# Attention and experts on one core: x loaded by columns, layer norm's scale applied to q on VectorE, no transposes of x

## What is computed

```
q = layernorm(x) @ W_q.T + b_q          k, v = ctx @ W_k.T + b_k, ctx @ W_v.T + b_v
attn = softmax(q k / 4) per head        x = x + (attn v) @ W_out.T + b_out
logits = layernorm(x) @ Wr + br         two best experts, gates = softmax of their logits
x = x + sum over the two of gate * ((silu(x_n W1a + b1a) * (x_n W1g + b1g)) @ W2 + b2)
```

## Time and profile before

| | us |
|---|---|
| median of 3 runs | 1176.52 (1175.81 to 1178.37) |
| the profiled execution | 1174.99 |
| its span, first to last instruction | 1173.2 |
| PE busy | 1136.0 (97%) |
| DVE busy | 941.5 (80%) |
| ACT busy | 774.8 (66%) |
| POOL busy | 597.5 (51%) |
| first scores (slot 0) | starts at 24.86 |
| slot 4 to slot 55 | 52.91 to 457.87 |
| expert part, all of it | about 530 to 1173 |

### The profile page before, as it was taken

One profiled execution on the slowest core, in us unless ns is written; L12 is line 12 of the kernel. 1 busy time (PEld: TensorE's weight loads), 2 busy tenths in 40 slices (PEclk: granted clock), 3 DMA queues, 4 the chain that ended last, 5 costly groups with the idle time before them and its releaser, 6 DMA issues. The chain is left out here.

```text
span 1173.2 us, 38427 instructions
## 1 busy us (share of the span) xinstructions
PE 1136.0 (97%) x12514; PEld 1018.2 (87%) x12515; DVE 941.5 (80%) x2949; ACT 774.8 (66%) x1635; POOL 597.5 (51%) x729
## 2 busy tenths in 40 slices
PE   6999999999999999988999999999999999999995
PEld 4677777777777777777999999999999999999995
DVE  6789999999999999898888877776776777677772
ACT  5677777777777776666766766666666666666652
POOL 6345677767766776595564333333333333333333
PEclk9999999999999999999999999999999999999998
DMA  5123333333333333536787776777777777767743
GB/s 191 36 74 94 110 106 100 113 113 104 104 109 113 111 102 105 188 127 215 191 221 201 200 212 171 217 195 190 189 210 200 172 198 210 192 172 214 194 109 68
DMA packets 106631, 180.18 MB, mean 154 GB/s; under 512 B 14400, under 2 KB 80128, under 8 KB 106368
## 3 DMA queue, kind: packets, MB, share of 16 engines
q1 hardware_dynamic: 74448, 136.54, 36.4%
q0 software_dynamic: 25584, 35.54, 16.0%
q10 hardware_dynamic: 6464, 6.36, 1.7%
HBM read 132.57 MB, written 45.29 MB: 152 GB/s over the span
## 5 line engine op out<-in xcount | busy, mean ns | idle before, releaser
L1782 POOL DMA_INDIRECT out_rows<-y_gated,block_tokens x114 | 187.2, 1642 | 257.3 <-DMA out_rows<-y_gated,block_tokens 107.4
L675 PE MATMUL bank<-block_T_hi,w_hi 128*128 128x256 f32 x912 | 261.1, 286 | 0.7 <-DVE block_T_lo L1397 0.7
L677 PE MATMUL bank<-block_T_hi,w_lo 128*128 128x256 f32 x912 | 256.1, 281 | 0.0
L676 PE MATMUL bank<-block_T_lo,w_hi 128*128 128x256 f32 x912 | 256.1, 281 | 0.0
L839 ACT ACTIVATE probs_T<-bank 128x512 f32<-128x512 f32 x256 | 132.1, 603 | 64.7 <-PE bank L512 64.7
L675 PEld LDWEIGHTS bank<-block_T_hi,w_hi 128*128 128x128 f32 x912 | 173.9, 191 | 0.9 <-DVE block_T_lo L1397 0.9
L676 PEld LDWEIGHTS bank<-block_T_lo,w_hi 128*128 128x128 f32 x912 | 173.2, 190 | 0.0
L677 PEld LDWEIGHTS bank<-block_T_hi,w_lo 128*128 128x128 f32 x912 | 172.9, 190 | 0.0
L1095 DVE TENSOR_REDUCE row_max<-bank 128x4 f32<-128x512 f32 x256 | 157.9, 675 | 13.0 <-PE bank L493 13.0
L1715 POOL DMA_INDIRECT routed_rows<-rows,dest_i x128 | 129.7, 1013 | 37.3 <-issue 33.4
L1380 DVE TENSOR_TENSOR w_lo<-w_raw,w_hi 128x1024 fp32r<-128x1024 f32 x114 | 134.1, 1218 | 6.2 <-ACT w_hi L940 6.2
(11 more groups left out here) (211 smaller groups left out, 2941.0 us busy)
## 6 DMA issues: line engine op xcount, KB each, us to landing
w_raw<-in_L_ffn_W SPq DMA_DIRECT2D x114, 512.0 KB, 4.7
half_w<-in_L_ffn_W SPq DMA_DIRECT2D x42, 512.0 KB, 5.6
block_rows<-routed_rows SPq DMA_DIRECT2D x57, 272.0 KB, 4.8
x_in<-in_x SPq DMA_DIRECT2D x64, 128.0 KB, 2.4
ctx_T<-in_ctx SPq DMA_DIRECT2D x16, 512.0 KB, 4.5
x_res<-in_x SPq DMA_DIRECT2D x64, 128.0 KB, 2.6
out_rows<-x SPq DMA_DIRECT2D x64, 128.0 KB, 2.3
w_lo<-in_L_ffn_W ACTq DMA_DIRECT2D x8, 512.0 KB, 4.4
```

Of the source, the lines that this page charges most:

```text
L675: mm(dst, w1h[k][:, c, at:at + P], xh[:, k, c, :], start=(c == 0), stop=False)
L676: mm(dst, w1h[k][:, c, at:at + P], xl[:, k, c, :], start=False, stop=False)
L677: last = mm(dst, w1l[k][:, c, at:at + P], xh[:, k, c, :], start=False, stop=(c == KC - 1))
L1782: nc.gpsimd.indirect_dma_start(out=out[:, :], out_offset=bass.IndirectOffsetOnAxis(ap=tk[:, u % U, t:t + 1], axis=0), in_=yg[:, u % 2, t, ...
```

## The change

- The host also lays x out by columns (`x_T`, as the context already is). Per group one DMA brings 512 KB (`load_xt`, q = 3). `xn`, `ln1_norm`, `to_T` and the transposes are gone. x by rows is still loaded, for the statistics alone.
- `xT_hi(g, c)`: two ACT casts of 128x512 per group (q = 3 and q = 1) in place of four of 128x256. `xT_lo(g, c)`: two DVE subtractions of 128x512, SBUF to SBUF, in slots q = 2 and 3, in place of four of 128x256.
- The mean is taken out of W_q once: two matmuls against a tile of 1/256, one DVE subtraction. rstd is applied behind the projection: `q_scaled(g, o)` on DVE, 128x512, PSUM times a row of rstd copied to all partitions, in slots q = 0 and 1; then ACT adds the bias in place at the end of the slot (`q_bias`).
- rstd goes through DRAM to become a row: SP stores 128x4 numbers at q = 0 (`store_rstd`) and loads them to 128 partitions at q = 1 (`load_rstd`). `rb` is then read with a step of four numbers (16 bytes).
- `rstd1` on POOL is one instruction instead of three. `ln1_stats` and `rstd1` stand at q = 2 and 3 instead of q = 1 and 3.
- `before()` is in another order on every engine.

```diff
+        def store_rstd(eng, g):
+            eng.wait_ge(s_rs1, 2 * (g + 1))
...
+            eng.dma_start(rr[g].rearrange("(p q) -> p q", p=P), rs1[:, g % 2, :]).then_inc(s_rst, 16)
+        def load_rstd(eng, g):
...
+            eng.dma_start(rb[:, g % 2, :], rr[g].rearrange("(o n) -> o n", o=1).to_broadcast([P, GB * P])).then_inc(s_rld, 16)
...
+                if t % GB == 0 and real(t + 2 * GB):
+                    store_rstd(sp, t // GB + 2)
+                if t % GB == 1 and real(t + 2 * GB):
+                    load_rstd(sp, t // GB + 2)
+                if t % GB == 3 and real(t + 4 * GB):
+                    load_xt(t // GB + 4)
...
-                if real(t + 9):
-                    pe.wait_ge(s_xl, t + 9)
-                    to_T(t + 9, bank[6])
...
+            def q_bias(g, o):
+                act.wait_ge(s_qm, 2 * g + o + 1)
+                dst = qT0[:, g % 3, :] if o == 0 else qT1[:, g % 2, :]
+                nc.scalar.activation(dst, dst, ACT.Identity, bias=bqc[:, o:o + 1]).then_inc(s_ev, 1)
...
+            def q_scaled(g, o, bk):
+                dve.wait_ge(s_qk, GB * g + o + 1)
+                dve.wait_ge(s_rld, (g + 1) * 16)
...
+                V.tensor_tensor(dst.rearrange("m (q p) -> m q p", q=GB), bk[:, :].rearrange("m (q p) -> m q p", q=GB),
+                                rb[:, g % 2, :].rearrange("m (p q) -> m q p", q=GB), ALU.mult).then_inc(s_qm, 1)
...
-                if real(t + 8):
-                    xT_lo(t + 8, bank[6])
+                if q < 2 and real(GB * (t // GB + 1)):
+                    q_scaled(t // GB + 1, q, bank[5])
+                if q >= 2 and real(GB * (t // GB + 2)):
+                    xT_lo(t // GB + 2, q - 2)
...
-                if t % 2 == 1 and real(t + 11):
+                if q == 2 and real(t + 10):
+                    ln1_stats(t + 10)
+                if q == 3 and real(t + 11):
                     ln1_stats(t + 11)
```

More of the change, by code:

```diff
@@ L451, in split3 @@
                 return last
-            def to_T(t, bk):
-                pe.wait_ge(s_xn, count(t))
-                for c in range(KC):
-                    last = nc.tensor.transpose(bk[:, c * P:(c + 1) * P], xn[:, t % LB, c * P:(c + 1) * P], ident)
-                last.then_inc(s_xT, 1)
             def qk_proj(g, o, bk):
@@ L536, in before @@
             def before():
-                pe.wait_ge(s_const, 16)
-                for q in range(GB):
-                    to_T(q, bank[q])
-                pe.wait_ge(s_wl, 2)
-                for o in range(4):
-                    qk_proj(0, o, bank[4 + o])
-                for q in range(GB):
-                    pe.wait_ge(s_xl, q + 1)
-                    to_T(GB + q, bank[q])
-                pe.wait_ge(s_wl, 4)
-                for q in range(GB):
-                    pe.wait_ge(s_ev, q + 1)
-                    v_proj(q, bank[4 + q])
-                pe.wait_ge(s_v, GB)
-                pe.wait_ge(s_xl, LB)
+                pe.wait_ge(s_zro, 1)
+                pe.wait_ge(s_wn[0], 16)
+                for c in range(KC):
+                    last = mm(bank[3][:, 0:D], avg[:], w_in[:, 0, c, :], start=(c == 0), stop=(c == KC - 1))
+                last.then_inc(s_wm, 1)
+                for o in range(4):
+                    if o % 2 == 0:
+                        pe.wait_ge(s_wl, o // 2 + 1)
+                    qk_proj(0, o, bank[4 + o])
+                pe.wait_ge(s_wl, 3)
+                for q in (2, 3, 0, 1):
+                    if q < 2:
+                        pe.wait_ge(s_qm, q + 1)
+                    else:
+                        pe.wait_ge(s_ev, q - 1)
+                    v_proj(q, bank[4 + q])
+                pe.wait_ge(s_const, 16)
             def squares_and_out(t):
@@ L604, in slot @@
                 if t == 0:
-                    to_T(LB, bank[6])
+                    pe.wait_ge(s_v, GB)
                     pe.wait_ge(s_bvr, 1)
+                    pe.wait_ge(s_wl, 4)
                     for c in range(KC):
@@ L891, in slot @@
                     nc.scalar.activation(nT[:].rearrange("p c n -> p (c n)"), bank[4][:, 0:D], ACT.Copy).then_inc(s_nT, 1)
-                if real(GB * g):
-                    qk_out(g, q, bank[5])
+                if real(GB * g) and q >= 2:
+                    k_out(g, q, bank[5])
                 if q == 0 and real(t - 8):
@@ L1191, in before @@
                 ln1_stats(2)
+                dve.wait_ge(s_wm, 1)
+                V.tensor_tensor(w_in[:, 0], w_in[:, 0],
+                                bank[3][:, 0:D].rearrange("p (o n) -> p o n", o=1).to_broadcast([P, KC, D]),
+                                ALU.subtract).then_inc(s_wc, 1)
+                for c in range(KC):
+                    xT_lo(0, c)
+                dve.wait_ge(s_wc, 1)
+                w_part_lo(0)
+                w_part_lo(1)
                 dve.wait_ge(s_const, 16)
@@ L1196, in before @@
                 last.then_inc(s_bke, 1)
-                w_part_lo(0)
-                w_part_lo(1)
-                for q in range(GB):
-                    xT_lo(q, bank[q])
+                w_part_lo(2)
                 ln1_stats(4)
-                w_part_lo(2)
                 ln1_stats(6)
+                for o in range(2):
+                    q_scaled(0, o, bank[4 + o])
+                for c in range(KC):
+                    xT_lo(1, c)
+                ln1_stats(LB)
                 w_part_lo(3)
-                ln1_stats(LB)
                 V.tensor_copy(tri_bf[:], consts[:, C_TRI:C_TRI + P])
@@ L1213, in before @@
                 last.then_inc(s_bvr, 1)
-                for q in range(GB):
-                    xT_lo(GB + q, bank[q])
                 ln1_stats(LB + 2)
```

187 lines of the change are left out of this document (102 added, 85 removed).

## The result

The changed kernel takes 1203.31 us (median of 4 runs, 1201.28 to 1204.49), the kernel before 1177.44 us (4 runs): 1.0222 times as long, 95% interval 1.0202 to 1.0242. The profiled execution took 1203.02 us, its span 1201.1 against 1173.2 us. So the span grew by 27.9 us; the prediction had put 3.9.

A forecast was written before the change was run, and what follows sets the result against it. It took PE's work and ACT's exponentials to end each slot together, with DVE nearly late at q = 0. -0.5 + 2.9 + 0.5 + 1.0 = +3.9 us on 1176.52 gave 1180.4 us, range 1175.5 to 1187.5.

The forecast's parts named there:

- PE's transposes, -0.01 us a slot: Steady slots: without PE's transposes the exponentials end the slot, 7.75 instead of 7.76 us; about -0.5 us over 51 slots.
- `q_scaled`, 0.69 us: DVE, slots q = 0 and 1: 689 ns for 128x512, 0.27 us more than what it replaces, if the step costs nothing.
- rival 1: Slots q = 0 and 1: the stepped rstd read makes `q_scaled` 1218 ns, +6 us, 1186.4 in all; chance 0.15.
- PE now has 0.46 us to give before `pv` 3: Slots q = 0 and 1: `q_scaled` delays x2, `v_proj` is 0.1 us late, and PE's spare time covers it: nothing.
- Slots q = 0, +0.24 at L507: Twelve slots q = 0 (8 to 52): DVE's maxima end 0.27 us later, L507 comes 0.24 us later; +2.9 us.
- Slots q = 1, "punctual" after losing the statistics: DVE, slots q = 1: about 1.5 us of statistics leave, 0.27 comes; its end is 1.2 us earlier, q = 2 starts punctual.
- q = 2 takes the statistics: DVE, slots q = 2: 1.5 us of statistics go into 1.60 us of idle time; taken as nothing.
- rival 2: SP's queue: maxima's rows come late behind the x_T load or rstd's store, +5.2 us, 1185.6 in all; chance 0.10.
- The start, +1.0 us: First slots: maxima of tile 0 at 26.1 to 28.4, so slots come 0 to 2.3 us later; +1.0 taken.
- Rival 3: The start gains what PE's first projection gains, some 3.5 to 4 us: 1175.6 in all; chance 0.14.
- Slots 56 and 57, +0.5: Slots 56 and 57 get two `q_scaled` where DVE is already late: about +0.5 us over three slots.
- Expert part, 0: Expert part at the end: same code and order, so no change, 0 us.

The follow-up runs named there:

- Experiment 5: Router's matmuls and ranks behind the transposed scores: changed kernel with rstd row ordered and POOL waiting, 1.0110; statistics moved too, 1.0109; kernel before, 1.0063.
- e2: Changed kernel, POOL in slots q = 0 waiting with its low part of the context until VectorE's four additions are done: 1.0152 times the kernel before.
- e11: Changed kernel with ACT copying the rstd row into order once per group and POOL waiting for the additions: 1.0139 times the kernel before, 1193.67 us.
- experiment 6: Addresses of W1's first-buffer tiles: kernel before with 64 bytes free ahead of them, 1.0053; changed kernel with them at the old addresses, 1.0084.
- e14: Kernel before with one unused 64-byte tile ahead of `w1_raw0`: 1.0053 times the kernel before.

## Why the prediction was wrong, point by point

- **PE's transposes, -0.01 us a slot.** Right, and with it the reading that the exponentials end the slot: q = 2 and 3 take 7.76 us, with the two waits of 0.3 us before `pv` 2 and 3. Experiment 5 adds that this holds for this order of PE only.
- **`q_scaled`, 0.69 us.** Mis-sized: 1.08, measured with and without the step (1076 and 691 ns). It lay between the bounds of 0.417 and 1.218, and I had taken "the row of its own size". This was rival 1's condition (over 0.95 us), chance 0.15. The Trainium skill ("Advanced Engine Details and Errata", SBUF Cachelines) speaks of a penalty where accesses each hit another 16-byte cacheline, and gives no figure; here it is 0.385 us over 512 numbers in each partition. (Rival 1's "0.65 us after `v_proj` could start" is 0.62 by the reckoning that made 0.27 us into 0.1 late; nothing hangs on it.)
- **What waits for it.** The step "PE now has 0.46 us to give before `pv` 3", so that only `v_proj` counts, failed. `pv` 0 waits for the addition of the logits (for q = 1 also for that of the ranks), which stands behind `q_scaled` on VectorE. Rival 1 priced the two slots at 0.42 us together with 0.65 us of lateness; slots q = 0 lost 0.2, and of the 0.94 us of slots q = 1 0.24 are lost behind L534.
- **Slots q = 0, +0.24 at L507.** The length was right by accident (7.96 us; "7.95 to 8.05"), its place wrong: L534 comes on time. q = 3 did not end 0.27 us later, because its last small instruction (`ln_var_eps`) takes 0.17 us and no longer 0.45: in the kernel before it stood at 333.61, just ahead of the row of 333.98 in the earlier trace rows, and ended with a POOL instruction (333.31 to 334.03).
- **Slots q = 1, "punctual" after losing the statistics.** This is the step that failed most: 11.9 of the 14.4 us. Its block transpose starts 1.59 us behind PE, for VectorE's slot q = 0 takes 8.79 instead of 7.14 us: 0.66 from `q_scaled` (1.08 - 0.42) and 0.92 from the two additions that stand behind POOL. That the statistics are gone from its own end does not help, since it is late at its start. No rival had the additions in it. One of these slots, 17, owes some 1.1 of its 2.05 us to the lower clock (below).
- **q = 2 takes the statistics.** Right: 7.76 us.
- **SP, the x_T load, the DMAs of rstd (rival 2).** Nearly right. In slots 4 to 55 one wait of L534 is for the DMA of the maxima, where the kernel before has none:

```profile
262.82 0.10 PEld L534 LDWEIGHTS bank<-minus_max_rows,ones_bf 2*128 2x128 bf16 x4 [0.67 <-DMA minus_max_rows<-minus_max_T]
```

This is slot 29, where the additions were short, so the slot's 8.53 us are in part the DMA's. e2 has one such wait (1.1 us) and e11 three (1.0 us together). Rival 2 had 0.4 us in one slot of four.
- **The start, +1.0 us.** Mis-sized: +3.5. Slot 0 began at 24.79, as before, but its maxima at 28.64 (forecast 26.1 to 28.4, before 26.02), and PE stood idle for 2.09 and 2.27 us, the second time until `q_scaled` of slot 0 had ended (31.78 + 1.04 = 32.82); slot 1 then began at the lower clock (granted 0.57 from 32.90 to 36.70) and took 8.20 us instead of 7.57:

```profile
24.79 0.77 PEld L520 LDWEIGHTS bank<-k_T_by_parity,q_T 32*128 32x128 f32 x16 [0.52 <-issue]
27.65 0.73 PEld L638 LDWEIGHTS bank<-w_in,ctx_by_token 128*128 128x128 f32 x4 [2.09 <-issue]
...
32.94 0.09 PEld L666 LDWEIGHTS bank<-id_bf,minus_max 128*32 128x32 bf16 x1 [2.27 <-issue]
33.11 1.08 PEld L520 LDWEIGHTS bank<-k_T_by_parity,q_T 32*128 32x128 f32 x16
...
35.01 0.33 PEld L483 LDWEIGHTS bank<-t_lo,w_hi 128*128 128x128 f32 x1
```

The load of 35.01 takes 0.33 us, that of an ordinary slot 0.19. Rival 3 (a quicker start) was wrong: PE's first projection starts at 13.33 against 13.26. Ahead of the maxima VectorE has two low parts of W_q of 1.09 and 1.76 us and two of x_T of 1.10 and 1.85, where such an instruction alone takes 0.68; POOL casts and splits the context at these times. The two casts that were to decide took 0.22 us each. What of this made the maxima late was not tested.
- **Slots 56 and 57, +0.5.** Mis-sized: +4.0 for 56 to 62. Slot 57 takes 10.18 us: PE waits 0.81 us twice, and what follows runs at the lower clock (granted 0.64 from 490.50 to 495.20; its 32 loads of L539 take 1.78 us instead of 1.09). Slot 17 did the same behind idle times of 0.70 and 0.57 us (0.58 from 166.00 to 169.90) and took 9.93 us.
- **Expert part, 0 ("same code and order").** Wrong: +5.9 us. The code is the same, the addresses are not (experiment 6).

The range ended at 1187.5, above rival 1 (1186.4), whose condition came true. What lies beyond it was in no rival. By estimates from the rows: the additions behind POOL (0.70 us of L534 in 12 slots, some 8 us), the addresses (5.9), the start's other 2.5, slot 1 with it, and the lower clock in slots 17 and 57 (some 2).

## What to carry to other kernels

List for an engine that waits every semaphore in the code of the waiting instruction, with what stands ahead of the one that sets it, and not only the releaser that the profile names: `pv` 0 had another wait that decided. An engine that is 80% busy with a queue in fixed order is the bound of single slots, so an instruction on VectorE that gets longer also moves others into the time of POOL, where two SBUF inputs make them wait. And when tiles are added or removed, compare addresses: time that is lost in code that was not touched may come from there.

## What the runs showed of the hardware

- A read with a step of 16 bytes: 1076 ns for 128x512 on VectorE against 691 ns without it, one operand in PSUM. ACT's copy of the same stepped row took 1.11 us (e11), its in-place addition of the bias to 128x512 0.70 (after).
- An addition of 8 numbers in each partition takes up to 724 ns where it meets POOL, 163 in the mean where it does not. An x_T low part (two SBUF inputs, which the old one from PSUM had not) takes up to 1.85 us in the start beside POOL, 0.68 in the slots.
- 64 bytes free ahead of a tile of weights change the step of matmuls from 0.1135 to 0.1185 us in a quarter of the up projections, and the kernel by 0.5% (e14).
- On three of the chips, from slot 10 on, where POOL's first scatter runs, ACT's first exponential starts 0.38 us later behind the same PE work: in slot 40 of the kernel before 5.66 us after its start instead of 5.28, and the slot takes 8.14 us. What ACT waits for there is open.
